# Two attention layers and two expert layers on one core: the order of TensorE's steps inside a turn is changed

## The chip, the core and the metric

The kernel runs on one core of a Trainium2 chip. The core has five engines with a queue each: TensorE (PE in the profile, its weight loads PEld), VectorE (DVE), ScalarE (ACT), GpSimd (POOL) and SyncE (SP), which issues the DMAs here. An engine takes its instructions in the order of its own program; engines wait for one another by semaphores. The metric is the device time of one execution in microseconds, the median of several runs.

## The reference, cut to what matters

```
x = x + attn_a(layernorm(x))       # 32 items of 256 tokens, width 128, 16 heads of 8; two scores masked
x = x + ffn(layernorm(x))          # 2 of 8 experts for each item, by a softmax over pooled tokens
x = x + attn_b(layernorm(x))       # the same shapes, no mask, no bias
x = x + ffn(layernorm(x))
# attention: q, k, v = projections; w = softmax(q k^T * scale); out = (w v) Wo
# ffn: h = gelu(x Wd + bd) * weight; out = h Wu + bu, summed over the two experts
```

## The kernel before

**Turns.** An item in one attention layer is a turn; there are 64, items 0 to 31 in the first layer and then again in the second. The program is one loop over steps n = -6 to 70, each of eight parts p = 0 to 7, written out for each engine by its own function step (steps, L388). A step works on several turns at once: the maxima of turn n+2, the exponentials and sums of turn n, the close of turn n-1, the projections of turns n+3 and n+4, the norm of turn n+5.

**Heads.** The 16 heads are taken in eight pairs. For a pair p, max_side(n+2, p) (TensorE, L851; four f16 matmuls at L836) makes scores with the tokens of the query on the partitions. VectorE reduces them to the negative maximum (L641). exp_side(n, p) (L860; four matmuls at L846) makes the scores again, transposed, with the maximum among the rows that are contracted, and ScalarE takes the exponential (L713). A pair is contracted over 32 rows of the array for each head; an even pair uses the first two of the four groups of 32 rows, an odd pair the last two (lanes_of, L354). Below, s4 is max_side of pair 4 and e4 is exp_side of pair 4; red4 is VectorE's reduction and exp4 ScalarE's exponential for them.

**The ring.** s and e results of all pairs, and two results of the expert layer (down and up), go to three buffers of PSUM in turn (ring, pair_of, L350). The order in which they take them is the list uses (L337 to L348): use number k takes buffer k modulo 3, and fill_pair (L362) makes TensorE wait until use k-3 has been read. In the kernel before, the list has s and e of a pair next to each other, which is not the order in which TensorE issues all of them.

**Sums.** weigh(n, g) (L815, the sixteen matmuls at L825; w0 to w3 below) multiplies four heads' exponentials with the values, and by a column of ones sums them; it needs exp of pairs 0 to 2g+1. w3 of turn n-1 comes in step n. ScalarE copies the four groups' result out (L740, oT), TensorE transposes it (L972), VectorE takes the reciprocal of the sums and multiplies (L657, L659: o), TensorE transposes that (L993, called oT2 below), ScalarE copies it (L783 or L785: onT), and the output projection with VectorE's addition to x (L629) closes the attention of the turn.

**One bank for the rest.** The projections, the transposes and the logits share one bank, m_bank. fill_m makes each of them wait until the one before has been read. The order of m_bank in a step is: transposed maxima (L946), q and k (qk), transposes of oT, value projection (v, L812; ScalarE copies it out at L777: vc), oT2, transposes of the normalised rows (L1005), output projection.

**TensorE's order around the change**, step n: p = 2: s2, qk. p = 3: s3, e2, e3, transposes of oT, w0. p = 4: s4, (down), v. p = 5: s5, e4, (up), oT2, e5, w1. p = 6: s6, transposes of the normalised rows, e6. p = 7: s7, w2, e7, output projection. Down and up, the products of the expert layer for four turns, come only in the sixteen steps of BURSTS (L273). ScalarE's order is exp3, (in a step of BURSTS the table of Gelu and four Gelus, L766), vc, exp4, onT, exp5. VectorE's is red3, reciprocal, o, red4, red5, statistics, (two additions of up's result to x, L672), (eight small operations of the experts' choice, L602 to L618), four aggregates (L579), red6. The choice falls in steps n = 11, 19, 27, 35, 43, 51, 55, 59, 63 and 67 (batch_at(n, 1)); in 19, 27, 35, 43 and 51 it meets a step of BURSTS.

Of the kernel before, what the change touches and what calls it, by code (L numbers as in the profile page):

```python
# [39 lines left out]
TURNS = 2 * ITEMS  # L40
# [21 lines left out]
def build(nc, x_dram_in, attn_w, attn_b, gate_w, down_w, down_b, up_w, up_b, tail_c, ident_c, iota_c, pick_c, out):  # L62
    ctx = ExitStack()
    with ctx:
# [206 lines left out]
        BATCHES = ((0, 8), (8, 8), (16, 8), (24, 8), (32, 8), (40, 8), (48, 4), (52, 4), (56, 4), (60, 4))  # L271
        LATE, FIRST_BY_VECTOR = 56, 56
        BURSTS = (19, 23, 27, 31, 35, 39, 43, 47, 49, 51, 54, 56, 58, 62, 66, 70)  # L273
        DOWN_AFTER, UP_AFTER = 3, 4
        MIXING = 12
        WHICH, NBEST = 3, 4
        SPLITS = 5
# [59 lines left out]
        uses = []  # L337
        for n in range(FIRST, LAST + 1):
            for p in range(PAIRS):
                if n + 2 >= 0 and n + 2 < TURNS:  # L340
                    uses.append(("scores", n + 2, p))
                if live(n):
                    uses.append(("exps", n, p))
                if p == DOWN_AFTER and n in BURSTS:
                    uses.append(("down", group_at(n), 0))
                if p == UP_AFTER and n in BURSTS:
                    uses.append(("up", group_at(n), 0))
        place = {use: k for k, use in enumerate(uses)}  # L348

        def pair_of(*use):  # L350
# [42 lines left out]
        with nc.Block() as block:  # L393
# [165 lines left out]
            def _(dve):  # L559
# [62 lines left out]
                def step(dve, n, p):  # L622
                    if n == FIRST + 2 and p == 0:
                        vector_opening(dve)
                    if p == 0 and live(n - 2):

                        dve.wait_ge(wo_done, (n - 2) + 1)
                        xs = x[:, tiles_of(n - 2), :]
                        nc.vector.tensor_tensor(xs, xs, m_bank[:, 0:TOKENS].rearrange("p (t d) -> p t d", t=TILES),  # L629
                                                ALU.add).then_inc(x_ready, 1)  # L630
                    if p == 0 and batch_at(n, 1) is not None:
                        best_of(batch_at(n, 1))
                    if live(n + 2):

                        i = (n + 2) % 2
                        if p == 0 and live(n):
                            dve.wait_ge(mparts_ready, n + 1)
                        dve.wait_ge(s_done, (n + 2) * PAIRS + (p + 1))
                        src = pair_of("scores", n + 2, p)[:, :, :].rearrange("p x (t k) -> p x t k", t=TILES)
                        dst = nmax[i][:, :, :].rearrange("p t (x j) -> p x t j", x=LANES)[:, lanes_of(p), :, p // 2]  # L640
                        nc.vector.tensor_reduce(dst, src, axis=AX.X, op=ALU.max, negate=True).then_inc(max_done, 1)  # L641
                    if p == 2 and live(n + 6):

                        for c, (start, _) in enumerate(CHUNKS):
                            if n + 6 == start:
                                dve.wait_ge(x_in[c], 16)
                        if n + 6 >= ITEMS:
                            dve.wait_ge(added, (n + 6 - ITEMS) // 2 + 1)
                        stats(n + 6, n % 2, raw_done)
                    if p == 3 and live(n - 1):  # L650

                        dve.wait_ge(on_done, (n - 1) + 1)
                        if live(n - 2):
                            dve.wait_ge(oT2_done, (n - 2) + 1)
                        both = m_bank[:, :].rearrange("p (m w) -> p m w", w=32)[:, :, 0:IN_SHARE * SUMS]
                        both = both.rearrange("p m (g e) -> p m g e", g=IN_SHARE)
                        nc.vector.reciprocal(rsum[:, :, :], both[:, :, :, HEAD]).then_inc(rsum_done, 1)  # L657
                        dve.wait_ge(rsum_done, (n - 1) + 1)
                        nc.vector.tensor_tensor(o[:, :, :].rearrange("p t (m g d) -> p (t m) g d", g=IN_SHARE, d=HEAD),  # L659
                                                both[:, :, :, 0:HEAD], rsum[:, :, :].unsqueeze(3).broadcast_to(  # L660
                                                    [P, TILES * HEADS // IN_SHARE, IN_SHARE, HEAD]), ALU.mult).then_inc(o_ready, 1)
                    if p == 5 and live(n - 2):
                        dve.wait_ge(x_ready, (n - 2) + 1)
                        stats(n - 2, 2 + n % 2, raw2_done)
                    if p == 5 and group_at(n) is not None:

                        group = group_at(n)
                        for half in range(2):
                            dve.wait_ge(up_done, 2 * group + half + 1)
                            xs = x[:, tiles_of(group * GROUP + 2 * half, 2), :]  # L670
                            src = pair_of("up", group, 0)[:, half, :].rearrange("p (t d) -> p t d", d=WIDTH)
                            nc.vector.tensor_tensor(xs, xs, src, ALU.add).then_inc(added, 1)  # L672
                    if p == 5 and batch_at(n, 1) is not None:
                        weights_of(batch_at(n, 1))
                        spread(batch_at(n, 1))
                    if p == 5 and live(n + 6):
                        aggregate(n, n + 6, n % 2, 0, raw_done, mv_done)
                    if p == 5 and live(n - 2):
                        aggregate(n, n - 2, 2 + n % 2, 1, raw2_done, mv2_done)
                    if p == 7:  # L680
                        for turn in PREPARED.get(n, ()):
                            if turn >= FIRST_BY_VECTOR:
                                if turn % GROUP == 0:
                                    experts[0] = experts_of(turn // GROUP, dve)
                                dve.wait_ge(weight_ready, batch_of(turn) + 1)
                                if turn >= DEEP:
                                    dve.wait_ge(up_done, (turn - DEEP) // 2 + 1)
                                z, col = turn % DEEP, turn - BATCHES[batch_of(turn)][0]
                                for k in range(TOP):
                                    half = slice(HIDDEN * k, HIDDEN * (k + 1))  # L690
                                    last = nc.vector.tensor_scalar(wu[z][half, :].unsqueeze(1),
                                                                   up_sb[half, bass.ds(experts[0][TOP * (turn % GROUP) + k], 1), :],
                                                                   weight[batch_of(turn) % 2][half, col:col + 1], None, ALU.mult)
                                last.then_inc(wu_ready, 1)
# [110 lines left out]
            def _(pe):  # L805
# [126 lines left out]
                def step(pe, n, p):  # L932
# [20 lines left out]
                    if p == 2 and live(n + 4):  # L953
                        wq, wk = projections[(n + 4) // ITEMS][0:2]
                        fill_m(pe, qk32_ready, (n + 4) + 1)
                        if n + 4 == 0:
                            pe.wait_ge(weights_ready, 1)
                        pe.wait_ge(xnT_ready, (n + 4) + 1)
                        for a, wmat in enumerate((wq, wk)):
                            last = by_columns(m_bank[:, a * TOKENS:(a + 1) * TOKENS], wmat, xnT[(n + 4) % 2][:, :],  # L960
                                              start=(a == 0), stop=(a == 1))
                        last.then_inc(qk_done, 1)
                    if p == 3 and live(n):
                        exp_side(n, 2)
                        exp_side(n, 3)
                    if p == 3 and live(n - 1):
                        fill_m(pe, o_ready, (n - 1) + 1)
# [7 lines left out]
                        weigh(n, 0)  # L975
                    if p == 4 and group_at(n) is not None:
                        down(group_at(n))
                    if p == 4 and live(n + 3):
                        wv = projections[(n + 3) // ITEMS][2]
                        fill_m(pe, v_ready, (n + 3) + 1)  # L980
                        for t in range(TILES):
                            last = by_columns(m_bank[:, t * P:(t + 1) * P], xnT[(n + 3) % 2][:, t * P:(t + 1) * P], wv,
                                              start=(t == 0), stop=(t == TILES - 1))
                        last.then_inc(v_done, 1)
                    if p == 5 and live(n):
                        exp_side(n, 4)
                    if p == 5 and group_at(n) is not None:
                        up(group_at(n))
                    if p == 5 and live(n - 1):
# [4 lines left out]
                        last.then_inc(oT2_done, 1)  # L994
                    if p == 5 and live(n):
                        exp_side(n, 5)
                    if p == 5 and live(n):
                        weigh(n, 1)
                    if p == 6 and (live(n + 5) or live(n - 3)):
                        fill_m(pe, *((yT_ready, (n - 3) + 1) if live(n - 3) else (xnT_ready, (n + 5) + 1)))  # L1000
                        pe.wait_ge(xy_ready, norm_steps(n))
# [72 lines left out]
```

## Time and profile before

| | us |
|---|---|
| median of 3 runs (940.13 to 941.30) | 940.43 |
| the profiled execution, its own time | 939.68 |
| its span, first to last instruction | 937.9 |
| TensorE busy in the span | 849.4 (91%) |
| VectorE busy | 786.9 (84%) |
| ScalarE busy | 765.2 (82%) |
| GpSimd busy | 537.2 (57%) |
| a step of the first layer without experts (261.63 to 274.06) | 12.43 |
| a step of the second layer without experts (711.38 to 723.72) | 12.34 |
| a step with down and up (341.64 to 358.08) | 16.44 |
| a step with down, up and the choice (286.48 to 303.99) | 17.51 |

A step is measured here from ScalarE's copy of one turn's sums (L740) to the next one's; the table of busy times by stretch gives TensorE's granted clock as 1.00 in all four. A timeline row gives start, length, engine, line, operation, what is written and read, how many instructions it joins, and in brackets the idle time of the engine before it with what ended it. The chain of work that ended last is followed back from the last instruction, at each step to what released it.

### The profile page before, as it was taken

Reading aid. Unit: us, or ns where it says so; the run is one execution under the profiler, and the core shown is the slowest. Engines: PE = TensorE matmul, PEld = TensorE weight load, DVE = VectorE, ACT = ScalarE, POOL = GpSimd, SP = SyncE. Lnnn points to the kernel's source line nnn. Section 1 sums busy time; section 2 is a strip of 40 time slices with the busy share of each in tenths; the row PEclk is TensorE's granted clock in tenths of the full one; section 3 lists DMA queues with packets and bytes.
Section 4 is the critical chain, followed back from the end, with each engine's and each line's share of the span. In section 5 each row is a group of like instructions: output and inputs, shape, how many; then the busy total and the mean of one; then the engine's idle time right before and its main releaser. Section 6 shows DMA issues by size and latency. Waiting matters only on the chain.

```text
span 937.9 us, 32135 instructions
## 1 busy us (share of the span) xinstructions
PE 849.4 (91%) x12592; PEld 427.6 (46%) x12592; DVE 786.9 (84%) x1410; ACT 765.2 (82%) x1305; POOL 537.2 (57%) x1086
## 2 busy tenths in 40 slices
PE   3699999999999999999999999999999998998875
PEld 1234444444445454454545445454554554554434
DVE  2889999999998988989898998989888888879533
ACT  2278888888888898888988888898888888887863
POOL 7335555545664666647565674657586485653442
PEclk9689999999999999999999999999999999999987
DMA  3354223222222122212222221222223132232001
GB/s 106 117 158 142 78 88 103 82 63 79 72 77 79 59 77 70 82 50 78 78 64 77 66 82 58 79 69 82 59 66 90 57 103 81 66 104 64 3 24 46
DMA packets 89862, 72.16 MB, mean 77 GB/s; under 512 B 5040, under 2 KB 72784, under 8 KB 89680
## 3 DMA queue, kind: packets, MB, share of 16 engines
q1 hardware_dynamic: 89280, 69.52, 24.7%
q8 instruction: 101, 1.65, 0.7%
q10 hardware_dynamic: 432, 0.59, 0.2%
q14 instruction: 49, 0.40, 0.1%
HBM read 39.68 MB, written 29.88 MB: 74 GB/s over the span
## 4 chain that ended last, share of the span: by engine, by line
PE 64%; ACT 16%; DVE 11%; issue 4%; DMA 1%; POOL 1%; POOLq 1%; SPq 0%; ACTq 0%; DVEq 0%
PE values_bank L825 24%; PE ring L836 10%; PE ring L846 9%; ACT probs L713 8%; DVE nmax L641 8%; PE m_bank L812 7%; PE m_bank L972 4%; PE m_bank L1005 3%; ACT values L777 2%; PE m_bank L993 2%; ACT oT L740 2%; PE ring L876 2%; PE ring L899 1%; ACT L713 1%; ACT hT L766 1%
## 5 line engine op out<-in xcount | busy, mean ns | idle before, releaser
L641 DVE TENSOR_REDUCE nmax<-ring 128x4 f32<-128x1024 f32 x512 | 604.6, 1219 | 70.5 <-PE ring L836 69.4
L713 ACT ACTIVATE probs<-ring 128x1024 f32<-128x1024 f32 x512 | 518.1, 1025 | 25.8 <-PE ring L846 20.7
L825 PE MATMUL values_bank<-probs,values 128*32 128x256 f32 x4096 | 278.9, 386 | 0.9 <-ACT probs L713 0.8
L836 PE MATMUL ring<-k_stack,q_stack 32*128 32x256 f16 x2048 | 201.3, 277 | 27.5 <-ACT probs L713 19.1
L535 POOL TENSOR_SCALAR xy<-x,mv,rstd 128x128 f32<-128x128 f32 x256 | 200.6, 793 | 7.9
L846 PE MATMUL ring<-q_stack,k_stack 32*128 32x256 f16 x2048 | 192.1, 273 | 12.1 <-DVE nmax L641 11.3
L513 POOL TENSOR_SCALAR mparts<-nmax 128x32 f16<-128x32 f32 x64 | 13.9, 218 | 290.5 <-DVE nmax L641 290.3
L825 PEld LDWEIGHTS values_bank<-probs,values 128*32 128x32 f32 x4096 | 118.9, 109 | 75.9 <-issue 36.4
L836 PEld LDWEIGHTS ring<-k_stack,q_stack 32*128 32x128 f16 x2048 | 57.4, 93 | 155.5 <-issue 71.5
L846 PEld LDWEIGHTS ring<-q_stack,k_stack 32*128 32x128 f16 x2048 | 62.9, 92 | 101.4 <-issue 48.1
L551 POOL TENSOR_TENSOR parts<-qk,parts 128x512 f16<-128x512 f32 x64 | 74.2, 1159 | 5.4
L528 POOL TENSOR_TENSOR rstd<-varp,minus_half 128x4 f32<-128x4 f32 (+1 forms) x72 | 69.5, 965 | 6.0
L570 DVE BATCH_NORM_STATS2 raw<-x 128x6 f32<-128x128 f32 x256 | 60.9, 280 | 3.8 <-DMA x<-in_x 3.7
L777 ACT COPY values<-m_bank 128x128 f32<-128x128 f32 x128 | 29.0, 281 | 41.5 <-PE m_bank L812 41.5
L790 ACT COPY xnT<-m_bank 128x256 f32<-128x256 f32 x64 | 23.8, 372 | 40.4 <-PE m_bank L1005 40.4
L629 DVE TENSOR_TENSOR x<-x,m_bank 128x256 f32<-128x256 f32 x64 | 27.0, 421 | 33.9 <-PE m_bank L812 33.9
L740 ACT COPY oT<-values_bank 128x512 f32<-128x512 f32 x64 | 37.5, 586 | 15.2 <-PE values_bank L825 15.2
L548 POOL TENSOR_SCALAR parts<-qk 128x512 f16<-128x512 f32 x64 | 39.5, 617 | 14.4 <-ACT qk L750 13.1
L1005 PE MATMUL m_bank<-ident,xy 128*128 128x128 f32 x256 | 45.0, 294 | 2.9 <-ACT qk L750 0.9
L972 PE MATMUL m_bank<-ident,oT 128*128 128x128 f32 x256 | 41.9, 286 | 2.5 <-ACT oT L740 1.3
L812 PE MATMUL m_bank<-xnT,wa 128*32 128x256 f32 x512 | 38.6, 424 | 2.3 <-DVE wb L258 1.7
L480 POOL COPY wu<-up_sb 64x128 f32 x112 | 32.5, 290 | 11.8 <-POOL wd L474 9.1
(118 smaller groups left out, 950.7 us busy)
## 6 DMA issues: line engine op xcount, KB each, us to landing
scratch<-parts SPq DMA_DIRECT2D x384, 64.0 KB
q_stack<-scratch SPq DMA_DIRECT2D x64, 256.0 KB, 2.7
k_stack<-scratch SPq DMA_DIRECT2D x64, 256.0 KB, 3.0
out<-x SPq DMA_DIRECT2D x16, 256.0 KB, 3.3
x<-in_x SPq DMA_DIRECT2D x3, 768.0 KB, 6.4
q_stack<-maxT SPq DMA_DIRECT2D x128, 8.0 KB
x<-in_x SPq DMA_DIRECT2D x1, 896.0 KB, 7.0
x<-in_x SPq DMA_DIRECT2D x1, 640.0 KB, 5.2
```

Source lines behind the costliest of these rows:

```text
L528: nc.gpsimd.tensor_tensor(rstd[i][:, both, :], varp[i][:, both, :], minus_half[:, both, :], ALU.pow).then_inc(rstd_done, 1)
L535: last = nc.gpsimd.tensor_scalar(xy[i][:, m, t, :], x[:, (turn % ITEMS) * TILES + t, :], mv[i][:, m, t, 0:1], rstd[i][:, m, t:t + 1], ALU. ...
L551: nc.gpsimd.tensor_tensor(parts[i][:, 1], qk32[i][:, :, :], parts[i][:, 0], ALU.subtract).then_inc(parts_ready, 1)
L570: last = nc.vector.bn_stats(raw[i][:, t, :], x[:, (turn % ITEMS) * TILES + t, :])
L641: nc.vector.tensor_reduce(dst, src, axis=AX.X, op=ALU.max, negate=True).then_inc(max_done, 1)
L713: nc.scalar.activation(probs[g % 2][:, c:c + 2, :, :], pair_of("exps", n, p)[:, :, :].rearrange("p x (k q) -> p x k q", k=TILES), ACT.Exp) ...
L812: last = nc.tensor.matmul(out[at], stationary[:, at], moving, start=start, stop=stop, skip_group_check=True)
L825: last = nc.tensor.matmul(values_bank[32 * c:32 * (c + 1), a * TOKENS:(a + 1) * TOKENS], values[turn % RING][:, k, PER_GROUP * g + c, :], ...
L836: last = nc.tensor.matmul(pair_of("scores", turn, p)[:, a, t * TOKENS:(t + 1) * TOKENS], q_stack[z][rows, p // 2, t * P:(t + 1) * P], k_st ...
L846: last = nc.tensor.matmul(pair_of("exps", turn, p)[:, a, k * TOKENS:(k + 1) * TOKENS], k_stack[r][rows, of // 2, k * P:(k + 1) * P], q_sta ...
L972: last = nc.tensor.transpose(m_bank[:, at:at + P], oT[(n - 1) % 2][:, a, t * P:(t + 1) * P], ident[:, :])
L1005: last = nc.tensor.transpose(m_bank[:, at:at + P], xy[(n + 5) % 2][:, m, t, :], ident[:, :])
```

## The change

The value projection moves behind s5 and e4, w1 moves ahead of up and oT2, e2 moves behind qk and so ahead of s3, and the ring's list now follows the order of issue: s4, then (down), s5, e4, (up), e5. Two of VectorE's four aggregates move from part 5 to part 3, between the reciprocal and the multiplication. Nothing is added or taken away.

```diff
-        DOWN_AFTER, UP_AFTER = 3, 4
+        DOWN_AFTER, UP_AFTER = 4, 4
+        EXPS_AT = ((0,), (1,), (2,), (3,), (), (4, 5), (6,), (7,))
...
-                if n + 2 >= 0 and n + 2 < TURNS:
+                if live(n + 2):
                     uses.append(("scores", n + 2, p))
-                if live(n):
-                    uses.append(("exps", n, p))
                 if p == DOWN_AFTER and n in BURSTS:
                     uses.append(("down", group_at(n), 0))
-                if p == UP_AFTER and n in BURSTS:
-                    uses.append(("up", group_at(n), 0))
+                for pair in EXPS_AT[p]:
+                    if live(n):
+                        uses.append(("exps", n, pair))
+                    if pair == UP_AFTER and n in BURSTS:
+                        uses.append(("up", group_at(n), 0))
...
@@ VectorE, step
+                    if p == 3 and not live(n - 1) and live(n + 6):
+                        aggregate(n, n + 6, n % 2, 0, raw_done, mv_done)
                     if p == 3 and live(n - 1):
...
                         nc.vector.reciprocal(rsum[:, :, :], both[:, :, :, HEAD]).then_inc(rsum_done, 1)
+                        if live(n + 6):
+                            aggregate(n, n + 6, n % 2, 0, raw_done, mv_done)
                         dve.wait_ge(rsum_done, (n - 1) + 1)
...
-                    if p == 5 and live(n + 6):
-                        aggregate(n, n + 6, n % 2, 0, raw_done, mv_done)
                     if p == 5 and live(n - 2):
@@ TensorE, step
+                    if p == 2 and live(n):
+                        exp_side(n, 2)
                     if p == 3 and live(n):
-                        exp_side(n, 2)
                         exp_side(n, 3)
...
-                    if p == 4 and live(n + 3):
+                    if p == 5 and live(n):
+                        exp_side(n, 4)
+                    if p == 5 and live(n + 3):
                         wv = projections[(n + 3) // ITEMS][2]
...
                     if p == 5 and live(n):
-                        exp_side(n, 4)
+                        weigh(n, 1)
                     if p == 5 and group_at(n) is not None:
                         up(group_at(n))
...
                     if p == 5 and live(n):
                         exp_side(n, 5)
-                    if p == 5 and live(n):
-                        weigh(n, 1)
```

## Rows read from the trace of the kernel before

**Rows 1.** The page, chain that ended last: shares of the span by engine.

```profile
PE 64%; ACT 16%; DVE 11%; issue 4%; DMA 1%; POOL 1%; POOLq 1%; SPq 0%; ACTq 0%; DVEq 0%
```

**Rows 2.** Timeline, TensorE, a first-layer step: start us, length us, engine, line, operation.

```profile
263.92 0.66 PE L972 MATMUL m_bank<-ident,oT 128*128 128x128 f32 x4
264.51 1.07 PE L825 MATMUL values_bank<-probs,values 128*32 128x256 f32 x16
265.51 0.39 PE L836 MATMUL ring<-k_stack,q_stack 32*128 32x256 f16 x4
265.83 0.64 PE L812 MATMUL m_bank<-wa,xnT 128*32 128x128 f32 x16
266.41 0.28 PE L836 MATMUL ring<-k_stack,q_stack 32*128 32x256 f16 x2
...
267.05 0.44 PE L993 MATMUL m_bank<-ident,o 128*128 128x128 f32 x2 [0.24 <-ACT values L777]
...
269.99 1.07 PE L825 MATMUL values_bank<-probs,values 128*32 128x256 f32 x16
...
272.82 0.23 PE L946 MATMUL m_bank<-identh,mparts 128*32 128x128 f16 x1
272.83 0.42 PE L825 MATMUL values_bank<-probs,values 128*32 128x256 f32 x3
```

**Rows 3.** Timeline, ScalarE, the same step.

```profile
263.38 0.49 ACT L750 ACTIVATE qk<-m_bank,bks 128x256 f32<-128x256 f32 x1
263.75 1.95 ACT L713 ACTIVATE probs<-ring 128x1024 f32<-128x1024 f32 x2
266.54 0.45 ACT L777 COPY values<-m_bank 128x128 f32<-128x128 f32 x2 [0.85 <-PE m_bank L812]
266.96 1.02 ACT L713 ACTIVATE probs<-ring 128x1024 f32<-128x1024 f32 x1
267.88 0.47 ACT L783 ACTIVATE onT<-m_bank,wa 128x256 f32<-128x256 f32 x1
268.24 1.02 ACT L713 ACTIVATE probs<-ring 128x1024 f32<-128x1024 f32 x1
```

**Rows 4.** Timeline, VectorE, the same step.

```profile
265.94 2.36 DVE L641 TENSOR_REDUCE nmax<-ring 128x4 f32<-128x1024 f32 x2 [0.26 <-PE ring L836]
...
268.61 0.37 DVE L579 BATCH_NORM_AGGREGATE mv<-raw 128x2 f32<-128x6 f32 x4
```

**Rows 5.** Timeline, TensorE, a second-layer step.

```profile
714.17 1.07 PE L825 MATMUL values_bank<-probs,values 128*32 128x256 f32 x16
...
719.65 1.07 PE L825 MATMUL values_bank<-probs,values 128*32 128x256 f32 x16
```

**Rows 6.** Timeline, ScalarE, the same second-layer step.

```profile
713.50 1.94 ACT L713 ACTIVATE probs<-ring 128x1024 f32<-128x1024 f32 x2
...
717.55 0.37 ACT L785 COPY onT<-m_bank 128x256 f32<-128x256 f32 x1
717.80 1.04 ACT L713 ACTIVATE probs<-ring 128x1024 f32<-128x1024 f32 x1
```

**Rows 7.** Timeline, VectorE, a step with down, up and the choice.

```profile
296.77 0.69 DVE L672 TENSOR_TENSOR x<-x,ring 128x512 f32<-128x512 f32 x1 [0.22 <-PE ring L899]
...
299.36 2.33 DVE L641 TENSOR_REDUCE nmax<-ring 128x4 f32<-128x1024 f32 x2
```

**Rows 8.** Timeline, TensorE, the same step.

```profile
300.61 0.39 PE L846 MATMUL ring<-q_stack,k_stack 32*128 32x256 f16 x4
```

**Rows 9.** Timeline, TensorE, a step with down and up, without the choice.

```profile
348.35 0.28 PE L836 MATMUL ring<-k_stack,q_stack 32*128 32x256 f16 x2
...
348.77 0.39 PE L891 MATMUL ring<-biasu_parts,pick 96*128 96x256 bf16 x2
...
354.01 1.07 PE L825 MATMUL values_bank<-probs,values 128*32 128x256 f32 x16
```

**Rows 10.** Timeline, ScalarE, the same step.

```profile
351.88 1.02 ACT L713 ACTIVATE probs<-ring 128x1024 f32<-128x1024 f32 x1
```

## The prediction

> **What bounds the kernel now.** I read the page's chain first, because it says which engine's work is late at the end: TensorE has 64% of it, ScalarE 16%, VectorE 11% [rows 1]. So the end is set by TensorE with handovers to ScalarE, and a change of TensorE's order can move it. Then I read one step of the first layer, engine by engine, with the clock set to zero where w0 starts (264.51). TensorE: s4 at 1.00, v at 1.32, s5 with e4 at 1.90, oT2 at 2.54 after 0.24 of idle time that ScalarE's copy of the values ended, w2 at 5.48 [rows 2]. ScalarE sits idle for 0.85 until v is there, and then runs vc, exp4, onT and exp5 without a pause: 2.03, 2.45, 3.37, 3.73 [rows 3]. VectorE waits 0.26 for s4 [rows 4]. All three wait for one another within a few tenths: no engine has a microsecond to give, and a step that gets shorter on TensorE soon meets ScalarE's chain. The second layer has the same 5.48 from w0 to w2 [rows 5], with a shorter onT [rows 6].
>
> **The change in a step without experts.** Four edits act together: the ring's list, v behind e4, w1 ahead of oT2, e2 ahead of s3. I walk the new order with the old durations.
> - e4 takes the buffer that e3 had, so it waits for exp3, where before it waited for s3's reduction. Behind it on TensorE stand v, w1 and oT2, and ScalarE's vc waits for v. exp3 ends at 1.19 (the two exponentials end at 265.70 [rows 3]). A handover from ScalarE to TensorE takes 0.06: vc ended at 266.99, oT2 began at 267.05 [rows 2, 3]. So e4 starts at 1.25, by when s4 and s5 have been issued.
> - v follows 0.32 later, as it followed s4 [rows 2]: 1.57, which is 0.25 later than before. This is the price of the move.
> - vc follows v by 0.71, exp4 vc by 0.42, onT exp4 by 0.92, exp5 onT by 0.36 [rows 2, 3]: 2.28, 2.70, 3.62, 3.98. exp5 ends 1.02 later, at 5.00.
> - s7 takes e5's buffer and waits for exp5, as w2 does anyway: s7 at 5.06, w2 0.32 later at 5.38. Before: 5.48. **Gain 0.10.**
>
> What hides the rest. TensorE: v, then w1 (1.00), then oT2. No row shows v followed by w1. The nearest rows on one side: v to s5 takes 0.58, which includes a gap before s5. On the other: L946 is followed by w3's first matmuls after 0.01, both in four groups of 32 columns, as v and w1 are [rows 2]. I take 0.46 for v (0.58 less 0.12), the value of the nearer kind. oT2 is then at 3.03, its result at 3.5, and onT could not start before 3.62 anyway: the cover is 0.10, and without it each 0.1 costs 0.1. The idle 0.24 ahead of oT2 is filled by w1, but ScalarE's queue takes its place: of 0.24 only 0.10 remains as gain.
>
> Here the Trainium skill bears on the price of v: "TensorEngine Tiling (Array Packing)", section Tiling Modes, Key Properties, says that a change of the tiling mode drains the array and a change of tile does not. The 0.01 agrees with it. By a drain there as well, the sum below would be 4.4 higher.
>
> s6 now waits for red5 in place of exp4. red4 and red5 ended at 3.79 [rows 4]; s6 at 3.85, its block 0.32, the transposes 0.59 (as L972 to w0 [rows 2]), e6 0.32: 5.08, under 5.38. Cover 0.30. s5 waits for red3 in place of exp3, long done. e2 ahead of s3 is costed at nothing: the transposes of oT start at 263.92, 0.05 after ScalarE's read of q and k ended at 263.87 [rows 2, 3], whatever stands before them; without that cover it would gain about 0.1. VectorE's two aggregates are half of 0.37, at most 0.19, ahead of the multiplication, which ended at 1.17 (0.26 before red4 [rows 4]); v, which needs it, comes at 1.57, so they are covered. GpSimd needs the other two as well, and those stay in part 5: no gain there. No DMA is moved, and GpSimd's and SyncE's programs stay. What follows w2 up to the next w0 keeps its order and its length.
>
> In the second layer exp3 ended at 1.27 [rows 5, 6], because exp2 came after s3. With e2 earlier I take e4 at 1.25, at the latest 1.33. Then onT at 3.62, only 0.25 before exp5 [rows 6], exp5 at 3.87, s7 at 4.95, w2 at 5.27: **gain 0.21**, at the least 0.13.
>
> **Steps with down and up.** Here v comes behind s5 and e4, then w1, then up: up moves by w1's 1.00, less 0.12 at v, less what up waited before (0.42 from s5 to up against 0.33 for such a pair of blocks [rows 9]; 0.09). So 0.79 later.
> - Without the choice, the late part is up, oT2, onT, exp5, w2. exp5 ran from 351.88 to 352.90 [rows 10]; with 0.06 and 0.32 w2 could have come at 353.28, and came at 354.01 [rows 9]. That slack is 0.73, so **0.06 is lost**.
> - With the choice, VectorE stands behind up: the second addition waited for it (0.22), and from there its queue ran full up to red6 at 299.36 [rows 7], which ends some 1.2 later; e7, on red6's buffer, starts at 300.61 [rows 8]. Nothing covers a delay of up here: 0.79, less some 0.1 for the two aggregates that have left this stretch: **0.69 is lost**. If VectorE's eight operations had slack it would be nothing.
>
> **The sum.** Of the 64 steps n = 0 to 63, 24 are first-layer steps without experts (n under 28, where turn n+4 is still in the first layer), 22 second-layer ones, 9 have down and up alone, 5 the choice as well, 4 the choice alone (left at zero). 24 x 0.10 = 2.4 and 22 x 0.21 = 4.6 are gained; 9 x 0.06 = 0.5 and 5 x 0.69 = 3.5 are lost: 3.0 gained. In the last turns there is no v left behind which w1 could hide, and exp5 comes later by most of a w1 once: I take 0.4 lost. Sum -2.6: 939.68 becomes 937.1 for the profiled execution, and the median of 940.43 becomes 937.8. Taking e4 at 1.33 in the second layer costs 1.8, and errors of 0.02 in each step 0.9: the forecast's own range is 936 to 939.5.
>
> **Rivals.**
> 1. The seam between v and w1 costs as much as that between v and s5 (0.12). First-layer steps lose 0.02 of their gain, since ScalarE hides the rest, second-layer ones about 0.10 (e5 then comes at 3.5 and exp5 after it), the 14 steps with up 0.12: 4.4 in all, 942.2. For it: each change between s blocks and full ones in the rows shows such a gap. Against: the 0.01 of L946 and w3.
> 2. **Slower:** TensorE held at e4. The wait for exp3 now stands ahead of v, and so of all ScalarE does from vc on. If exp3's release reaches e4 0.1 later than in my walk (past 1.35 in the first layer), the first layer's gain is gone, and 0.2 later the second's too; the steps with up still pay 4.0 and the last turns 0.4. That gives 944.8. It decides from about 0.06 lost per step. For it: ScalarE is already without idle time from vc to exp5. Against: exp2 and exp3 ran without a pause from 263.75.
> 3. **Faster:** the steps with the choice do not pay, because VectorE catches up before e7; or the second layer gains on both sides. Without those 3.5: 934.3. For it: VectorE is idle twice in a first-layer step. Against: no idle time between the second addition and red6.
> 4. The change does not do what it says: TensorE's 0.24 goes, but the wait comes back in full ahead of s7, in all steps, and the steps with up break even: 940.4.
>
> **How the numbers follow.** Chances: forecast 0.55, rival 1 0.10, rival 2 0.12, rival 3 0.13, rival 4 0.10. About 0.2% (1.9 us) is what a measurement of this kernel can tell from no change, so faster means under 938.5 and slower over 942.3. Four fifths of the forecast (0.44) and rival 3 are faster: 0.57. The rest of the forecast (0.11), rival 1 and rival 4 are the same: 0.31. Rival 2 is slower: 0.12. The range leaves out rival 2 and the far half of rival 3: 934.2 to 942.3.
>
> **What would show it.** Step lengths between ScalarE's copies of the sums: 12.43 to 12.33, 12.34 to 12.13, 16.44 to 16.5, 17.51 to 18.2. TensorE's wait ahead of oT2 for the values gone; new waits of an exp side for exp3 ahead of v, and of s7 for exp5. ScalarE's idle time ahead of vc up from 0.85 to about 1.1. VectorE's wait for up in the steps with the choice up by about 0.8. Wrong would be: w1 starting 0.58 after v (rival 1), first-layer steps of 12.43 or more (rival 2), steps with the choice under 17.6 (rival 3).

## The result and the profile after

The changed kernel takes 934.42 us (median of 9 runs, 931.88 to 938.33) where the kernel before takes 940.43 beside it (9 runs): a ratio of 0.9933, 95% interval 0.9918 to 0.9948, or 6.0 us less. Its profiled execution took 931.88 with a span of 930.1; that of before took 939.68 and 937.9, so the two traces differ by 7.8. The forecast was 937.8: the sign was right, the measured time lies just inside the range, and the gain is 2.3 times the forecast's 2.6.

The page's busy times and chain, which answer to [rows 1]:

```profile
PE 861.5 (93%) x12592; PEld 444.0 (48%) x12592; DVE 781.5 (84%) x1410; ACT 757.5 (81%) x1305; POOL 539.8 (58%) x1086
...
PE 66%; DVE 18%; issue 8%; ACT 4%; POOL 2%; DMA 1%; POOLq 0%; SPq 0%; DVEq 0%; ACTq 0%
```

ScalarE's share of the chain falls from 16% to 4% and VectorE's grows from 11% to 18%. In the table of waits, the 11.1 us of idle time of TensorE's matmuls ahead of oT2 for the values (47 times, up to 0.2) is gone. Three other rows say where the waiting is now (engine, line, releaser; us in total, times, longest):

```profile
ACT values L781 <- PE m_bank L816: 59.0, 51, 2.1
DVE x L678 <- PE ring L903: 30.0, 32, 4.5
ACT xnT L794 <- PE m_bank L1010: 4.5, 5, 1.7
```

Before they were 41.5 in 51, 13.6 in 19, and 40.4 in 64. ScalarE waits longer for v, as forecast; VectorE waits longer for up, as forecast; and ScalarE's wait for the transposes of the normalised rows, at the end of its queue vc to exp5, has nearly gone. The forecast had not looked at that one.

One first-layer step in TensorE's timeline, the counterpart of [rows 2]; w0 is at 261.21:

```profile
261.21 1.07 PE L829 MATMUL values_bank<-probs,values 128*32 128x256 f32 x16
262.21 0.40 PE L840 MATMUL ring<-k_stack,q_stack 32*128 32x256 f16 x8
262.45 0.39 PE L850 MATMUL ring<-q_stack,k_stack 32*128 32x256 f16 x4
262.77 0.64 PE L816 MATMUL m_bank<-wa,xnT 128*32 128x128 f32 x16
263.24 1.05 PE L829 MATMUL values_bank<-probs,values 128*32 128x256 f32 x16
264.21 0.44 PE L1000 MATMUL m_bank<-ident,o 128*128 128x128 f32 x2
...
266.18 0.39 PE L840 MATMUL ring<-k_stack,q_stack 32*128 32x256 f16 x4
266.50 1.07 PE L829 MATMUL values_bank<-probs,values 128*32 128x256 f32 x16
```

And ScalarE's, the counterpart of [rows 3], with the two copies of the sums between which the step is measured (258.33 to 270.57, 12.24):

```profile
258.33 0.59 ACT L744 COPY oT<-values_bank 128x512 f32<-128x512 f32 x1 [0.19 <-PE values_bank L829]
...
260.44 1.96 ACT L717 ACTIVATE probs<-ring 128x1024 f32<-128x1024 f32 x2
263.49 0.45 ACT L781 COPY values<-m_bank 128x128 f32<-128x128 f32 x2 [1.09 <-PE m_bank L816]
263.81 1.04 ACT L717 ACTIVATE probs<-ring 128x1024 f32<-128x1024 f32 x1
264.72 0.49 ACT L787 ACTIVATE onT<-m_bank,wa 128x256 f32<-128x256 f32 x1
265.08 1.05 ACT L717 ACTIVATE probs<-ring 128x1024 f32<-128x1024 f32 x1
...
270.57 0.59 ACT L744 COPY oT<-values_bank 128x512 f32<-128x512 f32 x1 [0.20 <-PE values_bank L829]
```

Against the forecast's walk, with w0 at zero:

| start | before | forecast | after |
|---|---|---|---|
| e4 | 1.91 | 1.25 | 1.24 |
| v | 1.32 | 1.57 | 1.56 |
| w1 | 3.23 | 2.03 | 2.03 |
| vc | 2.03 | 2.28 | 2.28 |
| **exp4** | 2.45 | **2.70** | **2.60** |
| oT2 | 2.54 | 3.03 | 3.00 |
| onT | 3.37 | 3.62 | 3.51 |
| exp5 | 3.73 | 3.98 | 3.87 |
| s7 | 5.16 | 5.06 | 4.97 |
| w2 | 5.48 | 5.38 | 5.29 |

Up to vc the walk holds to 0.01. At exp4 it is 0.10 too late, and what hangs on exp4 keeps 0.09 to 0.11 of it.

The second layer, TensorE and then ScalarE (w0 at 595.96):

```profile
595.96 1.07 PE L829 MATMUL values_bank<-probs,values 128*32 128x256 f32 x16
597.19 0.38 PE L850 MATMUL ring<-q_stack,k_stack 32*128 32x256 f16 x4
...
601.14 1.07 PE L829 MATMUL values_bank<-probs,values 128*32 128x256 f32 x16
```

```profile
595.03 1.97 ACT L717 ACTIVATE probs<-ring 128x1024 f32<-128x1024 f32 x2
```

Here w2 comes at 5.18 where the walk had 5.27 and before 5.48.

The lengths of the steps, summed by kind from the two traces:

| steps | forecast, each | forecast, sum | measured, each | measured, sum |
|---|---|---|---|---|
| first layer, without experts | -0.10 | -2.4 (24) | -0.19, two -0.05 | -4.0 (23) |
| second layer, without experts | -0.21 | -4.6 (22) | -0.21 (4), -0.30 (14), -0.08 to -0.26 (4) | -5.5 (22) |
| down and up | +0.06 | +0.5 (9) | 0.00 to -0.23 | -1.2 (9) |
| down, up and choice | +0.69 | +3.5 (5) | +0.62 to +0.64 | +3.2 (5) |
| choice alone, n = 11, 55, 59 | 0 | 0 | -0.14, -0.29, 0.00 | -0.4 (3) |
| last turn, n = 63 | +0.4 | +0.4 | +0.81 | +0.8 (1) |
| sum | | -2.6 | | -7.1 |

The step n = 0 lies ahead of the first copy. That stretch, the head, is 0.7 shorter, and what follows the last copy, the tail, is the same within 0.1: -7.8 in all.

### The profile page after: what moved, and what is told of

Its sections match the earlier page's. It is cut to its first block, busy times and chain, and to the rows that moved or that the text cites. A ratio compares the mean times of both kernels' runs of the same rounds, so it can differ in the third digit from the quotient of the medians.

```text
span 930.1 us, 32135 instructions
## 1 busy us (share of the span) xinstructions
PE 861.5 (93%) x12592; PEld 444.0 (48%) x12592; DVE 781.5 (84%) x1410; ACT 757.5 (81%) x1305; POOL 539.8 (58%) x1086
## 4 chain that ended last, share of the span: by engine, by line
PE 66%; DVE 18%; issue 8%; ACT 4%; POOL 2%; DMA 1%; POOLq 0%; SPq 0%; DVEq 0%; ACTq 0%
PE values_bank L829 19%; DVE nmax L643 14%; PE ring L840 11%; PE ring L850 10%; PE m_bank L816 9%; PE m_bank L977 4%; PE m_bank L1010 3%; PE ring L880 3%; PE ring L903 3%; ACT probs L717 2%; PE m_bank L950 1%; PE ring L895 1%; DMA wb<-in_attn_b 0%; DVE x L631 0%; DVE x L678 0%
## 5 line engine op out<-in xcount | busy, mean ns | idle before, releaser
L850 PE MATMUL ring<-q_stack,k_stack 32*128 32x256 f16 x2048 | 198.4, 273 | 14.1 <-DVE nmax L643 14.0
L840 PE MATMUL ring<-k_stack,q_stack 32*128 32x256 f16 x2048 | 183.2, 277 | 15.3 <-DMA k_stack<-scratch 5.1
L829 PEld LDWEIGHTS values_bank<-probs,values 128*32 128x32 f32 x4096 | 123.9, 109 | 63.8 <-issue 23.8
L840 PEld LDWEIGHTS ring<-k_stack,q_stack 32*128 32x128 f16 x2048 | 52.9, 93 | 115.4 <-ACT probs L717 41.2
L678 DVE TENSOR_TENSOR x<-x,ring 128x512 f32<-128x512 f32 x32 | 22.0, 688 | 30.0 <-PE ring L903 30.0
```

The costliest lines, as they stand in the source:

```text
L829: last = nc.tensor.matmul(values_bank[32 * c:32 * (c + 1), a * TOKENS:(a + 1) * TOKENS], values[turn % RING][:, k, PER_GROUP * g + c, :], ...
L840: last = nc.tensor.matmul(pair_of("scores", turn, p)[:, a, t * TOKENS:(t + 1) * TOKENS], q_stack[z][rows, p // 2, t * P:(t + 1) * P], k_st ...
L850: last = nc.tensor.matmul(pair_of("exps", turn, p)[:, a, k * TOKENS:(k + 1) * TOKENS], k_stack[r][rows, of // 2, k * P:(k + 1) * P], q_sta ...
```

## The experiments

Each starts from the changed kernel. Theory A is that of the walk: the gain comes from ScalarE's chain, exp4's distance from vc was mis-sized because exp4 had waited for e4's scores, and the rest of the sum holds. Its rivals are that another edit carries the surplus (the ring's list, the aggregates, w1's move by itself) or that the surplus is not in the steps at all.

**The changed kernel again, twice.** No edit.

> The changed kernel once more, for its spread. The first profiled execution took 931.88, the median of nine runs was 934.42. Theory A (the steps all have the lengths of the first profile, and what differs from run to run lies ahead of the first step or behind the last): step lengths 12.24, 12.04, 16.3 and 18.15 again, within 0.05, the head of 60.2 up to the first copy of sums longer. Theory B (the new order has waits that some runs meet and others don't): some of the steps without experts longer than 12.24 or 12.04, by up to 0.1 each.

Measured: 935.52 (6 runs) against 941.95 (17 runs), ratio 0.9944, 0.9926 to 0.9963. In the profiled execution the head is 61.13, the steps from the first copy to the last 836.17, the tail 33.40; in the trace shown above 60.17, 836.44 and 33.46.

> The changed kernel a third time, one look. Its two profiles so far have the same step lengths to 0.01 and times of 931.9 and 932.5, while other executions took up to 938.3. If this one is slow, its profile tells whether the time lies ahead of the first copy of sums (60.2 and 61.1 so far), behind the last (33.4), or in the steps (836.2 to 836.4).

Measured in one execution: 933.98, with 60.13, 836.19 and 35.87. The lengths of a step agree to 0.01 among the three traces nearly everywhere, so the surplus is in the steps and is no accident of one execution. What differs between executions lies in the head and the tail.

**w1 back behind oT2 and e5, in all steps.**

```
-                    if p == 5 and live(n):
-                        weigh(n, 1)
                     if p == 5 and group_at(n) is not None:
                         up(group_at(n))
...
                         exp_side(n, 5)
+                    if p == 5 and live(n):
+                        weigh(n, 1)
```

> The changed kernel with w1 behind oT2 and e5 in every step, as before; the rest of the change stays. Theory A (v behind e4 puts ScalarE's copy later, and only w1 covers it): oT2 waits for the copy again, about 0.5 to 0.6, and steps without experts take 12.6 and 12.5: some 949, slower than both. Rival (w1's place in those steps matters little, the gain is from the ring's list and e2): 12.25 and 12.05, the time that of the run before this one.

Measured: 948.98 (4 runs) against 941.95, ratio 1.0092, 1.0065 to 1.0119. Steps of 12.67 in the first layer and 12.55 in the second. TensorE's timeline, and then ScalarE's:

```profile
269.21 0.64 PE L816 MATMUL m_bank<-wa,xnT 128*32 128x128 f32 x16
270.43 0.44 PE L998 MATMUL m_bank<-ident,o 128*128 128x128 f32 x2 [0.57 <-ACT values L781]
```

```profile
269.93 0.45 ACT L781 COPY values<-m_bank 128x128 f32<-128x128 f32 x2 [1.09 <-PE m_bank L816]
270.25 1.04 ACT L717 ACTIVATE probs<-ring 128x1024 f32<-128x1024 f32 x1
```

Without w1 as cover, v's later place costs TensorE 0.57 of idle time ahead of oT2 in place of 0.24 [rows 2], and the kernel is slower than before by 7. exp4 follows vc by 0.32 here too: that distance goes with e4's early place, not with w1's.

**v back behind s4, so s5 and e4 behind v, w1 still ahead of oT2.**

```
-                    if p == 5 and live(n):
-                        exp_side(n, 4)
-                    if p == 5 and live(n + 3):
+                    if p == 4 and live(n + 3):
                         ...
+                    if p == 5 and live(n):
+                        exp_side(n, 4)
                     if p == 5 and live(n):
                         weigh(n, 1)
```

> The changed kernel with the value projection back behind s4, ahead of s5 and e4; w1 stays ahead of up and oT2. Theory A (w1 fills the wait for the values' copy, but e4 behind v comes late, so exp4 waits for e4 again, and w1 ahead of oT2 is then 1.0 on the way to exp5): 12.45 and 12.37, steps with the choice 18.3, some 948. Rival (the gain is from w1 ahead of oT2 alone): 12.25 and 12.05, some 934. exp4 after vc: 0.42 under A's reading of that distance as a wait for e4, 0.32 under a reading as ScalarE's own.

Measured: 944.26 (10 runs) against 941.95, ratio 1.0026, 1.0013 to 1.0039; steps of 12.43 and 12.30, steps with up and the choice 18.28. The time came out lower than the estimate of 948, and the second layer shorter by 0.07 a step. TensorE's timeline, then ScalarE's:

```profile
266.07 0.28 PE L850 MATMUL ring<-q_stack,k_stack 32*128 32x256 f16 x2
...
266.19 0.27 PE L850 MATMUL ring<-q_stack,k_stack 32*128 32x256 f16 x2
...
267.39 0.44 PE L1000 MATMUL m_bank<-ident,o 128*128 128x128 f32 x2
```

```profile
266.19 0.45 ACT L781 COPY values<-m_bank 128x128 f32<-128x128 f32 x2 [0.84 <-PE m_bank L816]
266.61 1.02 ACT L717 ACTIVATE probs<-ring 128x1024 f32<-128x1024 f32 x1
267.87 0.47 ACT L787 ACTIVATE onT<-m_bank,wa 128x256 f32<-128x256 f32 x1 [0.23 <-PE m_bank L1000]
```

With e4 behind v, exp4 is 0.42 after vc again, 0.15 after the end of e4's last matmul (266.19 and 0.27). w1 alone moves oT2 back, and onT then waits 0.23 for it. So neither move alone gains more than 0.04 in a plain step: v's move costs TensorE idle time, w1's costs ScalarE idle time, and together each fills the other's gap. What makes this kernel slower than the one before is the steps with the choice (0.77 each, five of them) and the last turn (0.8).

**e4 behind v alone, s5 left ahead of v.** This puts e4 late without pairing it with s5.

```
-                    if p == 5 and live(n):
-                        exp_side(n, 4)
                     if p == 5 and live(n + 3):
                         ...
+                    if p == 5 and live(n):
+                        exp_side(n, 4)
```

> The changed kernel with e4 behind the value projection (s4, s5, v, e4, w1, oT2, e5). It tests the reading of one distance: exp4 starts 0.42 after vc in the kernel before and 0.32 in the changed one. Theory A (0.32 is ScalarE's own, and 0.42 was the wait for e4's scores): e4 starts 0.55 to 0.6 after v again, and exp4 comes 0.42 or more after vc, with idle time of ScalarE between them that e4 ended; steps of 12.40 to 12.45. Rival (0.32 comes with another cause, such as the place of TensorE's writes): 0.32 again.

Measured in one execution: 949.52, against 940.40; steps of 12.42 and 12.30. TensorE's timeline, then ScalarE's:

```profile
267.95 0.64 PE L816 MATMUL m_bank<-wa,xnT 128*32 128x128 f32 x16
268.53 0.39 PE L850 MATMUL ring<-q_stack,k_stack 32*128 32x256 f16 x4
268.85 1.07 PE L829 MATMUL values_bank<-probs,values 128*32 128x256 f32 x16
```

```profile
268.67 0.45 ACT L781 COPY values<-m_bank 128x128 f32<-128x128 f32 x2 [0.86 <-PE m_bank L816]
269.02 1.02 ACT L717 ACTIVATE probs<-ring 128x1024 f32<-128x1024 f32 x1
270.33 0.47 ACT L787 ACTIVATE onT<-m_bank,wa 128x256 f32<-128x256 f32 x1 [0.28 <-PE m_bank L1000]
```

The distance from vc to exp4 is 0.35, neither the 0.42 of theory A nor the rival's 0.32. It is 0.10 after e4's end (268.53 and 0.39), where in the two kernels with s5 and e4 side by side it was 0.15. So exp4 does wait for e4 here, by 0.03. The other 0.05 lies in the ends of matmuls, which the trace models. The trace also records when each semaphore was raised, which the rows do not print, and those records agree: TensorE's signal that e4 is done comes 0.08 ahead of exp4's start here, 0.08 ahead of it in the kernel before and 0.08 in the one with v back; in the changed kernel it comes 0.94 ahead. Plain steps gain at most 0.04 over those of before, since onT waits for oT2 again. The steps with the choice take 18.59 where they took 17.51, and the nine with down and up alone are 2.5 longer in all: together these are the loss against the kernel before.

**The two aggregates back in part 5.**

```
-                    if p == 3 and not live(n - 1) and live(n + 6):
-                        aggregate(n, n + 6, n % 2, 0, raw_done, mv_done)
...
-                        if live(n + 6):
-                            aggregate(n, n + 6, n % 2, 0, raw_done, mv_done)
                         dve.wait_ge(rsum_done, (n - 1) + 1)
...
+                    if p == 5 and live(n + 6):
+                        aggregate(n, n + 6, n % 2, 0, raw_done, mv_done)
```

> The changed kernel with VectorE's two aggregates back in part 5. Theory A (they cost and bring nothing in a step without experts; in a step with the choice they stand behind up on VectorE): 12.24 and 12.04 stay, steps with the choice 18.25 in place of 18.15, in all some 0.5 us slower than the changed kernel, which can't be told in the time. Rival (the 0.1 a step that the forecast missed is theirs, the multiplication of o and red4 starting otherwise): 12.34 and 12.13, some 4 us slower.

Measured: 936.84 (10 runs) against 940.40 (13 runs), ratio 0.9962, 0.9941 to 0.9983. Plain steps are unchanged at 12.24 and 12.04; the five steps with up and the choice are 18.28 (0.13 longer), step 11 is 14.30 (0.13 longer). By the steps of the traces the edit is worth 0.7 (837.15 against 836.44; 1.0 against the changed kernel's other two traces); the medians lie 2.4 apart, more than that, with overlapping intervals.

**The ring's list as before.** Only the order in which uses take the three buffers goes back.

```
-        DOWN_AFTER, UP_AFTER = 4, 4
+        DOWN_AFTER, UP_AFTER = 3, 4
...
                     uses.append(("scores", n + 2, p))
+                if live(n):
+                    uses.append(("exps", n, p))
                 if p == DOWN_AFTER and n in BURSTS:
                     uses.append(("down", group_at(n), 0))
-                for pair in EXPS_AT[p]:
-                    if live(n):
-                        uses.append(("exps", n, pair))
-                    if pair == UP_AFTER and n in BURSTS:
-                        uses.append(("up", group_at(n), 0))
+                if p == UP_AFTER and n in BURSTS:
+                    uses.append(("up", group_at(n), 0))
```

> The changed kernel with the old list of the ring's uses (s and e of a pair next to each other, down ahead of s4). s5 then waits for exp3, e4 for red3, s6 for exp4, e5 for exp... of pair 4's buffer as before. Theory A (all of these end early enough; the gain is from the order of TensorE's work): 12.24 and 12.04 stay within 0.05, steps with up too, the time that of the changed kernel within 1 us. Rival (the ring's list brings part of the gain, above all s6 free of exp4 and s7 of the old wait): 12.35 or more.

Measured: 934.09 (5 runs) against 940.40, ratio 0.9926, 0.9900 to 0.9953. Steps of 12.25 and 12.04. The list by itself is worth nothing that can be measured here. Two steps of its trace, 55 and 56, are 1.1 and 0.4 longer; they are looked at below.

**w1 ahead of up and oT2 only where it gains:** late in the steps of BURSTS and in the last three turns, as before.

```
-                    if p == 5 and live(n):
+                    if p == 5 and live(n) and group_at(n) is None and live(n + 3):
                         weigh(n, 1)
...
                         exp_side(n, 5)
+                    if p == 5 and live(n) and not (group_at(n) is None and live(n + 3)):
+                        weigh(n, 1)
```

> The changed kernel, but in the 14 steps with up, and in the last three turns where no value projection is left, w1 stands behind oT2 and e5 as before. Theory A (up moved by w1's 1.0 is the whole loss in those steps): steps with the choice from 18.15 back to about 17.4, those with up alone from 16.3 to about 16.2, the last full turn 0.8 shorter; the others as they were; in all 4 to 5 us under the changed kernel, some 930. Rival (in those steps the loss is from the ring's new places, e6 waiting for up's addition and s7 for exp5): steps with the choice stay at 18.0 or more, no change of the time.

Measured: 929.49 (4 runs, 929.27 to 929.70) against 941.95, ratio 0.9877, 0.9859 to 0.9895: better than both kernels. Plain steps keep 12.24 and 12.04, steps with up and the choice take 17.37 in place of 18.15, and the last turn 9.65 in place of 10.46. The steps are 4.6 shorter in all than in the changed kernel: 3.9 from the five steps with the choice, 0.8 from the last turn, 0.4 from the steps with up, less 0.5 elsewhere. VectorE's timeline in the step with the choice, first the changed kernel's and then this one's:

```profile
292.76 0.69 DVE L678 TENSOR_TENSOR x<-x,ring 128x512 f32<-128x512 f32 x1 [1.04 <-PE ring L903]
293.87 0.69 DVE L678 TENSOR_TENSOR x<-x,ring 128x512 f32<-128x512 f32 x1 [0.42 <-PE ring L903]
```

```profile
292.10 0.69 DVE L678 TENSOR_TENSOR x<-x,ring 128x512 f32<-128x512 f32 x1 [0.27 <-PE ring L903]
293.21 0.69 DVE L678 TENSOR_TENSOR x<-x,ring 128x512 f32<-128x512 f32 x1 [0.43 <-PE ring L903]
```

The first addition's wait for up falls by 0.77, the step by 0.77. This shows, by undoing it, that the place of w1 ahead of up is what those steps pay for.

**e2 ahead of s3** has no run of its own; it is in all of these kernels. In the first layer the rows show nothing that it changed: w0 starts 2.88 after the copy of the sums (258.33 to 261.21; before 261.63 to 264.51), and exp3 ends 1.19 after w0, as before. In the second layer exp3 ends 1.04 after w0 (595.03 and 1.97) where it ended 1.27 before [rows 5, 6], and e4 starts at 1.23. With exp3's old end and a handover of 0.05, e4 would have come at about 1.32. So e2's move is worth some 0.1 in such a step; that is an estimate from these rows and not a measurement.

## Why the prediction was right, and where not

**The order and the seam: right.** v moved by 0.24 (0.25 forecast), and w1 follows v by 0.47 (0.46 forecast), so rival 1 falls. The sentence drawn from the Trainium skill, "TensorEngine Tiling (Array Packing)", Tiling Modes, Key Properties, that a change of the tiling mode drains the array and a change of tile doesn't, agrees with two rows: the same v is followed after 0.47 by w1, of its own tiling (128 x 32), and after 0.58 by e4, of another (32 x 128), in the kernel with e4 behind v. That the 0.11 between them is a drain no row shows.

**TensorE is not held at e4: right.** e4 starts at 1.24, 0.05 after exp3's end (260.44 and 1.96; 0.06 forecast). Rival 2 would have needed 1.35.

**exp4 after vc: the step that failed.** "vc follows v by 0.71, exp4 vc by 0.42" took 0.42 from [rows 3] as ScalarE's own distance between two instructions in its queue. The row has no idle time, so it looked so. But in that order e4 was issued beside s5, behind v:

```profile
266.42 0.28 PE L846 MATMUL ring<-q_stack,k_stack 32*128 32x256 f16 x2
266.53 0.27 PE L836 MATMUL ring<-k_stack,q_stack 32*128 32x256 f16 x2
266.54 0.27 PE L846 MATMUL ring<-q_stack,k_stack 32*128 32x256 f16 x2
```

These are TensorE's rows of before. e4 ends at 266.81 and exp4 starts at 266.96, while vc, which is two copies in 0.45, runs until 266.99 by its row. The start of exp4 was set by e4, whose signal came 0.08 ahead of it, and vc's length covered the wait, so no idle time appears. Moved ahead of v, e4 is long done, and 0.32 is left. The kernels bear it out: 0.32 with e4 ahead of v (with w1 early or late), 0.42 and 0.35 with e4 behind it. The walk moved e4 and yet kept a distance that e4 had made. With 0.32 in it, the walk gives 5.28 for w2 (measured 5.29), and 5.17 in the second layer (5.18). There two small misses cancel: vc comes 0.03 earlier than walked, and exp5 follows onT by 0.30 in place of 0.25.

In the sum this term is 0.09 for most plain steps: -0.19 in place of -0.10 in 21 of the first layer, and -0.30 in place of -0.21 in 14 of the second. That is 3.0 of the 4.5 between the forecast's -2.6 and the -7.1 of the traces; the steps with down and up are 1.7 more, and the other groups and the last turn nearly cancel. Four steps of the second group, n = 28, 29, 30 and 32, gained 0.21 only because they were put in the wrong group: their onT is still that of the first layer (0.36 ahead of exp5, not 0.25), so the right forecast for them was -0.10, and the missed 0.10 made it up.

**Steps with down and up: the same error again.** TensorE's up moved by 0.77 (0.79 forecast). ScalarE's timeline of the changed kernel in step 23, to be read against [rows 10]:

```profile
348.62 0.47 ACT L787 ACTIVATE onT<-m_bank,wa 128x256 f32<-128x256 f32 x1 [0.59 <-PE m_bank L1000]
348.99 1.02 ACT L717 ACTIVATE probs<-ring 128x1024 f32<-128x1024 f32 x1
```

onT to exp5 is 0.37. Before, it was 0.45 (351.43 to 351.88), since e5's block ended at 351.83. So exp5 moved by 0.69, not by the whole 0.77, which is 0.04 less than the slack of 0.73 [rows 9, 10]: -0.05 where +0.06 was forecast. In the second layer the distance falls further, from 0.45 to 0.33 in step 39. And up, which starts 5.02 after w0 in each of these steps now, had started there at 4.30 (step 39) to 4.39 (step 56) and not at 4.25 as in step 23, so it moved by less. These two give the -0.14 of step 39 and the -0.23 of step 56; why up had been later there was not looked into.

**The steps with the choice alone** were left at zero without a walk. Steps 11 and 55 gain 0.14 and 0.29, about what a plain step of their layer gains; why step 59 gains nothing is open.

**Steps with the choice: right.** +0.64 against +0.69. The chain is the one forecast: up, two additions, eight small operations, red6, and e7 waiting 0.65 for it. The aggregates' 0.1 measured 0.13. Rival 3 said that these steps don't pay and put the time at 934.3, all but the measured 934.42. It is refuted by the step lengths and by the kernel with w1 late in those steps: the time alone would have confirmed the wrong mechanism.

**The last turn: half.** +0.4 was taken, +0.8 measured. TensorE's timeline there, and ScalarE's:

```profile
889.80 1.07 PE L829 MATMUL values_bank<-probs,values 128*32 128x256 f32 x16 [0.68 <-ACT probs L717]
890.80 0.44 PE L1000 MATMUL m_bank<-ident,o 128*128 128x128 f32 x2
```

```profile
888.75 1.90 ACT L717 ACTIVATE probs<-ring 128x1024 f32<-128x1024 f32 x2
891.27 0.37 ACT L789 COPY onT<-m_bank 128x256 f32<-128x256 f32 x1 [0.62 <-PE m_bank L1000]
```

With no s, no projections and no v left between, w1 waits 0.68 for exp3 and only then runs its 1.00, with oT2 queued behind it. ScalarE waits 0.62 for oT2. The kernel with w1 late there has 9.65 again. The forecast's 0.4 was taken and not walked, and here w1 costs twice that.

**From steps to medians: partly open.** The steps give -7.1, the medians -6.0 and -6.4. Heads of 60.1 to 62.9 and tails of 33.4 to 35.9 over the traces of this study span more than that difference; there is one trace of before only, so how its head and tail are spread is not known.

## What to carry to other kernels

A start-to-start distance between two instructions of one engine is the engine's own only if the second one's other inputs were ready; where they come late but within the first one's length, the trace shows no idle time and the distance still contains a wait. Before a walk reuses such a distance, look at when each input of the second instruction ended, above all when the change moves that input. And two moves of which one loses alone and the other gains next to nothing can gain together, if each fills the idle time that the other opens: an undo of one part at a time then shows a loss for each, and only the pair tells what either is worth.

## What the hardware showed unexpectedly

Steps repeat to 0.01 us nearly everywhere from execution to execution, while among the changed kernel's three traces the head differs by 1.0 and the tail by 2.5. TensorE's granted clock differs there too. In the tail the two go together: 33.46 us at a mean clock of 0.72 in the first trace, 33.40 at 0.74 in the second and 35.87 at 0.67 in the third, and TensorE is busy for 18.88, 18.84 and 21.29 of it. In the head they do not: the mean clock from 40 to 50 us is 0.73, 0.71 and 1.00 with heads of 60.17, 61.13 and 60.13, and 0.50, the lower of its two levels (1.2 GHz) throughout, with 60.83 in the trace of before.

From the first copy of the sums to the last the clock is 1.00 (2.4 GHz) in nine of the ten traces. The exception is the kernel with the old ring list, from 787 to 793 us. Its row of the table by stretch (us, busy times of the five queues, clock, DMA), and then the changed kernel's for the same work:

```profile
787.00:793.00 6.00, 5.80 (x87) 2.85 (x85) 4.87 (x7) 4.15 (x8) 4.57 (x9) 0.72 0.70 200
```

```profile
786.00:792.00 6.00, 5.80 (x99) 2.96 (x97) 5.95 (x8) 5.26 (x9) 4.43 (x9) 1.00 0.67 207
```

0.72 is a mean of both levels. Ahead of it TensorE had been idle for 1.13 at e7, waiting for red6; in the changed kernel it was idle for 0.97 at the same place, and the clock stayed:

```profile
786.74 0.39 PE L849 MATMUL ring<-q_stack,k_stack 32*128 32x256 f16 x4 [1.13 <-DVE nmax L642]
...
789.07 1.91 PE L828 MATMUL values_bank<-probs,values 128*32 128x256 f32 x13
```

```profile
785.88 0.39 PE L850 MATMUL ring<-q_stack,k_stack 32*128 32x256 f16 x4 [0.97 <-DVE nmax L643]
...
788.15 1.03 PE L829 MATMUL values_bank<-probs,values 128*32 128x256 f32 x13
```

The same thirteen matmuls take 1.91 in place of 1.03, and the steps 55 and 56 are 1.1 and 0.4 longer. It was seen in one trace. The length of that idle time alone does not explain it: in the kernel with w1 late in the steps of BURSTS TensorE was idle for 1.18 at the same place (until 781.98), in the kernel before for 1.32 (until 858.44), and in both the clock stayed at 1.00. The cause is open.
